# A Mamba layer between two expert layers: the convolution's input copied by ScalarE from its matmul bank to a padded SBUF buffer

## The chip, the cores and the metric

One core of a Trainium2 chip runs the whole kernel. The time is the device time of one execution, in microseconds (us). TensorE (PE) does the matmuls, VectorE (DVE) and ScalarE (ACT) the work on their results, GpSimd (POOL) some of the elementwise work, and SyncE (SP) issues most DMAs. Each engine runs its own instructions in order and waits on semaphores for the others.

## The reference, cut to what matters

Eight sequences of 256 tokens with 256 features pass through an expert layer, a Mamba layer with a small gated MLP, and the expert layer again. The part that the change touches is the depthwise causal convolution inside the Mamba layer, four taps over time for each of 512 channels:

```
zxbcdt = einsum('bld,pd->blp', h, in_proj_w)
z, x, B, C, dt = split(zxbcdt, ...)
x = repeat_kv(x)                          # 128 -> 512 channels
xc = conv(x over time, conv_w, 4 taps, 3 zeros in front) # per channel
x = silu(xc + conv_b)
# then, token by token: state = exp(dt*A)*state + dt*x*B ; y = sum(state*C)
```

## The kernel before

**Layout.** Features and channels lie on the 128 partitions, the 256 tokens of a sequence along the free dimension. The 512 channels are four groups of 128; everything before the scan is done in two halves (0 and 1) of two groups, so one instruction often covers 128x512 numbers and one tap of the convolution 128x256.

**Steps and items.** The program is unrolled into steps t = -1 to 9. A step holds, for different sequences at once, an MLP (`gum`, line 850, with `down`, line 889), the expert layer (`g` and `u`, lines 808 to 810, `down`), the scan of sequence t-1 in 32 units, and the front of the next sequence (norms, projections, convolution, softplus). In the text "the MLP stretch" is the part of a step in which `gum` items run, 35 to 52 us long, and "the expert stretch" the rest, 109 to 162 us from step 2 to step 8. The front's half 0 of the next sequence (`("x", 0, "next")`) is placed in the expert stretch, half 1 (`("x", 1, "own")`) in the following MLP stretch. There are 16 such halves; step 1 does both halves of the first sequence as well.

**The order.** `items_of(t)` makes one list of items for a step and every engine walks through this list, doing its part of each item (`late_order` holds some items back on DVE and POOL). `merge` interleaves two lists: each item gets the position (lengths of the items ahead of it) / (total length of its list), and the two lists are sorted by it. The lengths are in `SPACE` (scan units against the front) and `WEIGHT` (matmul-heavy items against all that). `near` moves an item that frees a bank ahead if too many bank uses would pass; in this list it moves only the item `om`, never a convolution item.

**Side banks.** PE writes the small products into three PSUM banks (`side`), used in turn; `last_use` makes PE wait until the third use back is over, which is what `USES` and `ENDED_BY` say. For a scan unit there are two uses: `ub` (line 983, freed by the scan, line 1352) and `unit` (line 986, freed by the multiply, line 1358). For the projection x (line 956) the use ends when all eight taps are done (semaphore `conv`).

**The convolution.** DVE does the taps straight from the bank, four in item `xc` (tap 3 without shift, line 1283, and tap 2, line 1288) and four in `xd` (taps 1 and 0, line 1288), two groups each. A late tap covers only the columns that it reaches (255, 254 or 253). Tap results accumulate in `xs`. Then ACT does the tanh of the silu (`xt`, line 1094).

**Scan units on DVE and POOL.** Item `ub` multiplies (line 1340) and `unit` scans (line 1352) and multiplies (line 1358). POOL adds each unit's result to a sum (line 1478, 128x512); behind the last unit of a group (units 7, 15, 23, 31) it makes two narrower adds more (lines 1481 and 1484, 128x256). POOL also does two multiplies for each chunk of the expert layer (`by_u`, line 1457, and `by_comb`, line 1465).

Of the kernel before, what the change touches and what calls it, by code (L numbers as in the profile page):

```python
# [33 lines left out]
P = 128  # L34
SEQ, BATCH, DM = 256, 8, 256
# [64 lines left out]
    "rt2": {"side_filled": 1, "comb_ready": 1},  # L100
    "z": {"side_filled": 1, "z_tanh": 1},
    "zm": {"z_done": 1},
    "x": {"side_filled": 1},
    "xc": {"conv": TAPS},
    "xd": {"conv": TAPS},
    "xt": {"x_tanh": 1},
# [92 lines left out]


FILLS = ("n1", "n2", "rt1", "rt2", "z", "x", "split", "dt", "ub", "unit", "outp")
ENDS = {"x": "xd", "ub": "unit", "outp": "om", "z": "zm", "split": "sr", "n1": "nc"}


def near(items):

    out, done, open_for = [], set(), {}

    def emit(it):
        if it in done:  # L210
            return
        if it[0] == "xd":
            emit(("xc",) + it[1:])
        fills = it[0] in FILLS and kind_of(it) != "n1r"
        if fills:
            for end in [e for e, n in open_for.items() if n >= SIDES - 1 and e != it]:
                emit(end)
            for end in open_for:
                open_for[end] += 1
        open_for.pop(it, None)  # L220
        done.add(it)
        out.append(it)
        if fills and it[0] in ENDS:
            open_for[(ENDS[it[0]],) + it[1:]] = 0

    for it in items:
        emit(it)
    return out
# [28 lines left out]
def items_of(t):  # L257
# [61 lines left out]
    if ln2:  # L319
# [9 lines left out]
          **{(k, w): x for w in ("lnO", "rmsO") for k, x in (("n1", 2), ("nc", 2), ("n2", 3), ("nm", 2))},  # L329
          **{(k, i, "own"): x for k, i, x in (("split", 0, 2), ("x", 0, 2), ("sr", 0, 2), ("dt", 0, 2), ("xt", 0, 2),  # L330
                                              ("split", 1, 2), ("sr", 1, 2), ("z", 0, 2), ("sp", 0, 2))}}
SPACE = {"n1": 1.4, "nc": 5, "n2": 3, "nm": 4, ("n1", "rms1"): 4, ("nm", "rms1"): 5, "rq": 0.75, "split": 1.4, "sr": 2, "sl": 2, "x": 1.4, "xc": 2, "xd": 2, "xt": 2,
         "xm": 2, "z": 1.4, "zm": 2, "dt": 2, "sp": 2, "sp_dt": 2, "sp_x": 1, "y0": 1, "ub": 2, "unit": 2, "rt1": 2,
         "yz": 0.1, "outp": 4, "om": 2, ("yz", JC - 1): 2, ("n1", "rms2"): 2}

# [91 lines left out]
def late_order(items):  # L427

    out, held, left = [], None, 0
    for it in items:  # L430
# [6 lines left out]
        else:  # L437
# [6 lines left out]
USES = {  # L444
    "side": {"n1c": [("centered", 1)], "n2": [("logged", 1)],
             "rt1": [("rt_exp", 1)], "rt2": [("comb_ready", 1)],
             "z": [("z_done", 1)], "x": [("conv", TAPS)],
             "split": [("part_rest", 1)],
             "dt": [("dt_pre", 4)], "ub": [("scanned", 1)],
             **{name: [("read_out", 1)] for name in ("unit_first", "unit", "unit_last")},  # L450
# [2 lines left out]
            "cmb": [("comb_copied", 1)]},  # L453
}

ENDED_BY = {"x": "xd", "g": "by_g", "ub": "unit", "outp": "om", "z": "zm", "split": "sr", "n1": "nc"}
BANKS = {"side": SIDES, "gub": GUBS}


# [34 lines left out]
def macaron_kernel(nc, d):  # L494
# [12 lines left out]
    with ctx:  # L507
        def sb(name, shape, dt=F32):
            return ctx.enter_context(nc.sbuf_tensor(name, shape, dt))
# [59 lines left out]
        lbuf = sb("lbuf", [P, 2, SEQ])  # L569
        tmp = sb("tmp", [P, 2, SEQ])  # L570
        dtr = sb("dtr", [P, SEQ])
        decays = sb("decays", [P, 2, 2, SEQ])
        decay = [decays[:, i, :, :] for i in range(2)]

# [99 lines left out]
        def pair(b):  # L674
            return b[:, :].rearrange("p (h s) -> p h s", h=2)
# [328 lines left out]
        def _(act):  # L1004
# [5 lines left out]
            def do(s, it):  # L1010
# [59 lines left out]
                elif kind == "y0":  # L1070
                    act.wait_ge(sem["dtx"], s.count("dtx", ("sp_x",) + it[1:], 1))
                    for j in range(2 * it[1], 2 * it[1] + 2):
                        A(y[:, j, :], xs[:, j, :], ACT.Copy, scale=vecs[:, j, 0:1]).then_inc(sem["y_init"], 1)
                elif kind == "carry":
                    act.wait_ge(sem["normed"], s.count("normed", it, 0))
                    A(hn[:], hn_next[:], ACT.Copy).then_inc(sem["carried"], 1)
                elif kind == "rt1":
                    act.wait_ge(sem["side_filled"], s.count("side_filled", it, 1))
                    A(e_sc[:], s.side_of(it)[:, 0:TT * EXPERTS].rearrange("p (a e) -> p a e", a=TT),
                      ACT.Exp, scale=-1.0).then_inc(sem["rt_exp"], 1)  # L1080
                elif kind == "z":
                    act.wait_ge(sem["side_filled"], s.count("side_filled", it, 1))
                    j = 2 * it[1]
                    if (least := s.count("y_gated", it, 0)) is not None:
                        act.wait_ge(sem["y_gated"], least)
                    A(z2[:, j:j + 2, :], pair(s.side_of(it)), ACT.Tanh,
                      scale=0.5).then_inc(sem["z_tanh"], 1)
                elif kind == "xt":
                    act.wait_ge(sem["conv"], s.count("conv", ("xd",) + it[1:], TAPS))
                    if (least := s.count("part_lo", it, 0)) is not None:  # L1090
                        act.wait_ge(sem["part_lo"], least)
                    if (least := s.count("x_done", it, 0)) is not None:
                        act.wait_ge(sem["x_done"], least)
                    A(tmp[:], xs[:, 2 * it[1]:2 * it[1] + 2, :], ACT.Tanh).then_inc(sem["x_tanh"], 1)
                elif kind == "split":
                    act.wait_ge(sem["side_filled"], s.count("side_filled", it, 1))
                    if (least := s.count("spread", it, 0)) is not None:
                        act.wait_ge(sem["spread"], least)
                    b = pair(s.side_of(it))
                    if it[1] == 0:  # L1100
                        A(dtr[:], b[:, 1, :], ACT.Copy).then_inc(sem["part_hi"], 1)
                        A(parts[:, 0, 0, :], b[:, 0, :], ACT.Copy).then_inc(sem["part_hi"], 1)
                    else:
                        for h in range(2):
                            A(parts[:, 0, h, :], b[:, h, :], ACT.Copy).then_inc(sem["part_hi"], 1)
                elif kind == "sr":
                    n = 1 if it[1] == 0 else 2
                    act.wait_ge(sem["part_rest"], s.count("part_rest", it, 1))
                    A(parts[:, 1, 0:n, :], tmp[:, 0:n, :], ACT.Copy).then_inc(sem["part_mid"], 1)
                elif kind == "dt":  # L1110
                    act.wait_ge(sem["side_filled"], s.count("side_filled", it, 1))
                    for last_read in ("dt_fix", "decay", "dtx"):
                        if (least := s.count(last_read, it, 0)) is not None:
                            act.wait_ge(sem[last_read], least)
                    b = pair(s.side_of(it))
                    for h in range(2):
                        j = 2 * it[1] + h
                        A(ubuf[:, h, :], b[:, h, :], ACT.Abs, bias=vecs[:, j, 1:2]).then_inc(sem["dt_pre"], 1)
                        A(dts[:, j, :], b[:, h, :], ACT.Relu, bias=vecs[:, j, 1:2]).then_inc(sem["dt_pre"], 1)
                    act.wait_ge(sem["dt_pre"], s.count("dt_pre", it, 4))  # L1120
                    A(ubuf[:], ubuf[:], ACT.Exp, scale=-1.0).then_inc(sem["dt_exp"], 1)
                elif kind == "sp":
                    act.wait_ge(sem["dt_exp"], s.count("dt_exp", it, 0))
                    if (least := s.count("dt_fix", it, 0)) is not None:
                        act.wait_ge(sem["dt_fix"], least)
                    A(lbuf[:], ubuf[:], ACT.Ln, bias=1.0).then_inc(sem["dt_ln"], 1)
                elif kind == "ub":
                    u = it[1]
                    j, p = u // PAIRS, u % PAIRS
                    if u % (UNITS // 2) == 0:  # L1130
                        act.wait_ge(sem["dt_fix"], s.count("dt_fix", it, 0))
                    if u == 0 and s.n == 2:
                        act.wait_ge(a_ready, 1)
                    if (least := s.count("scanned", it, 1, back=2)) is not None:
                        act.wait_ge(sem["scanned"], least)
                    for h in range(2):
                        n = 2 * p + h

                        A(decay[u % 2][:, h, 1:SEQ], dts[:, j, 1:SEQ], ACT.Exp,  # L1139
                          scale=a_neg[:, j, n:n + 1]).then_inc(sem["decay"], 1)  # L1140
# [5 lines left out]
        def _(dve):  # L1146
# [3 lines left out]
            v.memset(marks[:, :, 1:2], -2.0).then_inc(zeroed, 1)  # L1150
            for i in range(2):
                v.memset(decay[i][:, :, 0:1], 0.0).then_inc(zeroed, 1)
            dve.wait_ge(zeroed, 5)
            dve.wait_ge(a_exp, 1)
            v.tensor_scalar(a_neg[:], a_neg[:], -1.0, None, ALU.mult).then_inc(a_ready, 1)
            v.tensor_copy(sc[:, :, EXPERTS:SCW], marks[:]).then_inc(a_ready, 1)
# [4 lines left out]
            def do(s, it):  # L1161
# [104 lines left out]
                                           ALU.add, ALU.mult).then_inc(sem["z_done"], 1)  # L1266
                elif kind in ("xc", "xd"):

                    of = ("x",) + it[1:]
                    dve.wait_ge(sem["side_filled"], s.count("side_filled", of, 1))  # L1270
                    if kind == "xd":
                        dve.wait_ge(sem["conv"], s.count("conv", ("xc",) + it[1:], TAPS))
                    taps = range(TAPS - 1, TAPS // 2 - 1, -1) if kind == "xc" else range(TAPS // 2 - 1, -1, -1)
# [3 lines left out]
                    for k in taps:  # L1277
                        for h in range(2):
                            j, late = 2 * it[1] + h, TAPS - 1 - k
                            o, i = xs[:, j, late:SEQ], pair(s.side_of(of))[:, h, 0:SEQ - late]  # L1280
                            w = vecs[:, j, 3 + k:4 + k]
                            if late == 0:
                                v.tensor_scalar(o, i, w, vecs[:, j, 2:3], ALU.mult,
# [280 lines left out]
```

## Time and the profile before

| | |
|---|---|
| median of 3 runs | 1781.56 us (1778.46 to 1782.3) |
| the profiled execution | 1783.27 us, span 1781.4 us |
| PE busy | 1551.8 us, 87% of the span |
| DVE busy | 1265.5 us, 71% |
| POOL busy | 988.8 us, 56% |
| ACT busy | 843.5 us, 47% |
| granted TensorE clock, mean | 0.958 |

The span is the time from the first to the last instruction of the program. An engine's busy time is an average over stretches with different limits, so the wait views and the timelines of single stretches say more than the shares.

### The profile page before, as it was taken

To read this page: it belongs to the slowest core of one execution; us is meant where nothing else is said; L and a number is where in the kernel's file an instruction comes from. 1 tells how busy PE (TensorE), PEld (TensorE's weight loads), DVE (VectorE), ACT (ScalarE), POOL (GpSimd) and SP (SyncE) were. 2 spreads that over 40 slices of the span, in tenths; PEclk is the share of its full clock that TensorE was granted. 3 is DMA by queue.
4 is the path that set the end of the run, shared out by engine and by line. 5 is a ranking of instruction groups with operands and counts; after the bars stand their busy time and mean duration, and the time that the engine had idled before them with its cause. 6 is when DMAs were issued, how large, how long until landed. Compare 5 with 4: busy or idle time off the path is not lost. (4 is left out here: it accounts for less than half of the span.)

```text
span 1781.4 us, 22496 instructions
## 1 busy us (share of the span) xinstructions
PE 1551.8 (87%) x7088; PEld 1165.3 (65%) x7088; DVE 1265.5 (71%) x2067; ACT 843.5 (47%) x1692; POOL 988.8 (56%) x1048
## 2 busy tenths in 40 slices
PE   5998887887899889888998799879987998889979
PEld 4665554546566567666776677667765776667868
DVE  4553587876868788968797879778977787777321
ACT  4443454543555346535553466346634564444323
POOL 1663354654767457636665566447644666458525
PEclk9999999999999999999999999999998999889989
DMA  4565221123323232423232333233322333233434
GB/s 161 205 217 192 75 95 50 63 77 103 133 90 113 97 121 92 138 88 116 95 126 96 98 115 128 89 104 116 126 95 73 124 114 113 80 112 131 133 100 149
DMA packets 73430, 202.35 MB, mean 114 GB/s; under 512 B 10049, under 2 KB 22561, under 8 KB 72929
## 3 DMA queue, kind: packets, MB, share of 16 engines
q1 hardware_dynamic: 65120, 175.75, 29.6%
q0 software_dynamic: 8192, 25.17, 4.6%
q8 instruction: 57, 0.93, 0.2%
q14 instruction: 61, 0.49, 0.1%
HBM read 175.46 MB, written 25.43 MB: 113 GB/s over the span
## 5 line engine op out<-in xcount | busy, mean ns | idle before, releaser
L1478 POOL TENSOR_TENSOR ring<-ring 128x512 f32<-128x512 f32 x192 | 256.9, 1338 | 378.9 <-DVE ring L1358 378.6
L808 PE MATMUL gub<-x_hi,wr 128*128 128x384 f32 (+2 forms) x1040 | 428.9, 412 | 29.1 <-DVE hid L1175 22.4
L889 PE MATMUL acc<-hid,w_down 128*128 128x384 f32 (+2 forms) x1040 | 408.1, 516 | 15.6 <-POOL hid L1457 15.5
L1457 POOL TENSOR_TENSOR hid<-hid,u_sb 128x384 f32<-128x384 f32 (+2 forms) x260 | 292.0, 1123 | 182.2 <-ACT u_sb L1041 168.0
L810 PE MATMUL gub<-x_hi,wr 128*128 128x384 f32 (+2 forms) x1040 | 370.0, 356 | 0.0
L809 PE MATMUL gub<-x_lo,wr 128*128 128x384 f32 (+2 forms) x1040 | 369.8, 356 | 0.0
L1352 DVE TENSOR_TENSOR_SCAN ring<-decays,side 128x512 f32<-128x512 f32 x256 | 310.4, 1213 | 40.1 <-ACT decays L1139 37.3
L1051 ACT ACTIVATE hid<-gub 128x384 f32<-128x384 f32 (+2 forms) x324 | 156.6, 483 | 365.9 <-PE gub L850 189.5
L1041 ACT ACTIVATE u_sb<-gub 128x384 f32<-128x384 f32 (+2 forms) x260 | 132.2, 508 | 336.6 <-PE gub L810 336.5
L1465 POOL TENSOR_TENSOR hid<-hid,weight 128x384 f32<-128x384 f32 (+2 forms) x240 | 267.6, 1116 | 29.6 <-ACT weight L1031 15.0
L889 PEld LDWEIGHTS acc<-hid,w_down 128*128 128x128 f32 x1040 | 185.7, 192 | 110.9 <-issue 41.8
L808 PEld LDWEIGHTS gub<-x_hi,wr 128*128 128x128 f32 x1040 | 202.1, 194 | 64.5 <-issue 37.4
L1340 DVE TENSOR_TENSOR side<-dtx,side 128x512 f32<-128x512 f32 x256 | 176.7, 690 | 93.5 <-PE side L983 93.1
L1139 ACT ACTIVATE decays<-dts,a_neg 128x255 f32<-128x255 f32 x512 | 228.5, 497 | 0.1
L809 PEld LDWEIGHTS gub<-x_lo,wr 128*128 128x128 f32 x1040 | 202.7, 195 | 20.0 <-issue 6.3
L810 PEld LDWEIGHTS gub<-x_hi,wr 128*128 128x128 f32 x1040 | 201.2, 193 | 13.8
L1175 DVE SCALAR_TENSOR_TENSOR hid<-hid,gub 128x384 f32<-128x384 f32 (+2 forms) x260 | 149.1, 573 | 85.7 <-ACT hid L1051 85.6
L1358 DVE TENSOR_TENSOR ring<-ring,side 128x512 f32<-128x512 f32 x256 | 176.2, 688 | 46.1 <-PE side L986 22.6
L983 PE MATMUL side<-bst,sel_b 96*128 96x256 bf16 x512 | 100.9, 279 | 63.4 <-DVE ring L1352 46.2
L850 PE MATMUL gub<-xn_mlp,wm_gu 128*128 128x256 f32 x512 | 129.3, 402 | 4.7 <-DMA wm_gu<-in_w_mlp 3.5
L956 PE MATMUL side<-rn,w_in 128*128 128x256 f32 x448 | 118.1, 411 | 15.5 <-DVE ring L1352 13.4
L983 PEld LDWEIGHTS side<-bst,sel_b 96*128 96x128 bf16 x512 | 40.3, 99 | 133.0 <-DVE ring L1352 62.0
(117 smaller groups left out, 1856.8 us busy)
## 6 DMA issues: line engine op xcount, KB each, us to landing
wr<-w_halves SPq DMA_DIRECT2D x234, 512.0 KB, 3.3
wm_gu<-in_w_mlp POOLq DMA_DIRECT2D x64, 256.0 KB, 3.1
w_halves<-wr SPq DMA_DIRECT2D x26, 512.0 KB, 3.2
wm_down<-in_w_mlp POOLq DMA_DIRECT2D x64, 128.0 KB, 2.7
w_raw<-in_w_gu SPq DMA_DIRECT2D x26, 256.0 KB, 3.7
rows<-parts SPq DMA_DIRECT2D x16, 384.0 KB, 2.3
cst<-rows SPq DMA_DIRECT2D x48, 128.0 KB, 2.5
xin<-in_x SPq DMA_DIRECT2D x8, 256.0 KB, 3.0
```

Of the source, the lines that this page charges most:

```text
L808: mm(out, w[:, 0, half, k, :], x_hi[:, k, a:b], start=(k == 0), stop=False)
L809: mm(out, w[:, 0, half, k, :], x_lo[:, k, a:b], start=False, stop=False)
L810: last = mm(out, w[:, 1, half, k, :], x_hi[:, k, a:b], start=False, stop=(k == KC - 1))
L889: last = mm(acc[k][:, a:b], w, h[:, a:b], start=(c == 0), stop=(c == (MLP_CHUNKS if mlp else FFN_CHUNKS) - 1))
L1051: A(hid[c % HSLOTS][:, a:b], s.gub_of(it)[:, a:b], ACT.Tanh, scale=0.5).then_inc(sem["tanh_done"], 1)
L1139: A(decay[u % 2][:, h, 1:SEQ], dts[:, j, 1:SEQ], ACT.Exp, scale=a_neg[:, j, n:n + 1]).then_inc(sem["decay"], 1)
L1340: v.tensor_tensor(b, twice(dtx[:, j, :]), b, ALU.mult).then_inc(sem["driven"], 1)
L1352: v.tensor_tensor_scan(w.rearrange("p h s -> p (h s)"), decay[u % 2][:, :, :].rearrange("p h s -> p (h s)"), s.side_of(ub)[:, :], 0.0, ALU ...
L1358: v.tensor_tensor(w, w, pair(s.side_of(it)), ALU.mult).then_inc(sem["read_out"], 1)
L1457: nc.gpsimd.tensor_tensor(h, h, u_sb[c % USLOTS][:, a:b], ALU.mult).then_inc(sem["hidden"], 1)
L1465: nc.gpsimd.tensor_tensor(h, h, weight[c // 3 % CSLOTS][:, a:b], ALU.mult).then_inc(sem["weighted"], 1)
L1478: add(ysum, ysum, ring[:, ring_at(it)], ALU.add).then_inc(sem["y_sum"], 1)
```

## The change

ACT gets a new part for item `x`: it copies the bank, 128x512, to a new SBUF buffer `xpad` of 259 columns for each group, whose first three columns are set to zero once at the start. The bank's use ends with this copy (semaphore `x_padded`). DVE waits for the copy and not for the matmul, and takes all eight taps from `xpad`, each over all 256 columns with a shifted start. In the planner the length of `x` in `SPACE` goes from 1.4 to 2, and `xd` is no longer an item that `near` knows as the end of `x`.

```
-    "x": {"side_filled": 1},
+    "x": {"side_filled": 1, "x_padded": 1},
...
-ENDS = {"x": "xd", "ub": "unit", "outp": "om", "z": "zm", "split": "sr", "n1": "nc"}
+ENDS = {"ub": "unit", "outp": "om", "z": "zm", "split": "sr", "n1": "nc"}
...
-        if it[0] == "xd":
-            emit(("xc",) + it[1:])
...
-SPACE = {... "x": 1.4, ...
+SPACE = {... "x": 2, ...
...
-             "z": [("z_done", 1)], "x": [("conv", TAPS)],
+             "z": [("z_done", 1)], "x": [("x_padded", 1)],
...
-ENDED_BY = {"x": "xd", "g": "by_g", "ub": "unit", "outp": "om", "z": "zm", "split": "sr", "n1": "nc"}
+ENDED_BY = {"g": "by_g", "ub": "unit", "outp": "om", "z": "zm", "split": "sr", "n1": "nc"}
...
+        xpad = sb("xpad", [P, 2, SEQ + TAPS - 1])
...
+                elif kind == "x":
+                    act.wait_ge(sem["side_filled"], s.count("side_filled", it, 1))
+                    if (least := s.count("conv", it, 0)) is not None:
+                        act.wait_ge(sem["conv"], least)
+                    A(xpad[:, :, TAPS - 1:], pair(s.side_of(it)), ACT.Copy).then_inc(sem["x_padded"], 1)
...
-            dve.wait_ge(zeroed, 5)
+            v.memset(xpad[:, :, 0:TAPS - 1], 0.0).then_inc(zeroed, 1)
+            dve.wait_ge(zeroed, 6)
...
-                    dve.wait_ge(sem["side_filled"], s.count("side_filled", of, 1))
+                    dve.wait_ge(sem["x_padded"], s.count("x_padded", ("x",) + it[1:], 1))
...
-                            o, i = xs[:, j, late:SEQ], pair(s.side_of(of))[:, h, 0:SEQ - late]
+                            o, i = xs[:, j, :], xpad[:, h, k:k + SEQ]
```

## Rows read from the trace of the kernel before

**Rows 1.** The page: busy us of each engine, share of the span, instructions.
```profile
PE 1551.8 (87%) x7088; PEld 1165.3 (65%) x7088; DVE 1265.5 (71%) x2067; ACT 843.5 (47%) x1692; POOL 988.8 (56%) x1048
```

**Rows 2.** Windows: stretch; its length; busy PE, PEld, DVE, ACT, POOL; clock; DMA.
```profile
160.00:403.30 243.30, 193.30 (x757) 126.52 (x757) 178.72 (x272) 120.09 (x225) 118.52 (x95) 0.94 0.24 79
...
606.70:644.30 37.60, 31.17 (x139) 24.96 (x140) 29.52 (x57) 14.24 (x30) 15.75 (x30) 0.92 0.25 77
```

**Rows 3.** Waits: who <- whom: us in total, times, longest.
```profile
DVE xs L1283 <- PE side L956: 20.8, 9, 2.8
...
PE side L986 <- DVE xs L1288: 10.8, 8, 2.4
...
PE side L967 <- DVE xs L1288: 2.4, 2, 1.2
```

**Rows 4.** Instructions that touch the tile xs: the taps, ns min/median/max.
```profile
L1288 DVE SCALAR_TENSOR_TENSOR xs<-side,vecs,xs x96: 468/473/481, 189.0 to 1530.6; 128x255 f32<-128x255 f32 x32, 128x254 f32<-128x254 f32 x32, 128x253 f32<-128x253 f32 x32
L1283 DVE TENSOR_SCALAR xs<-side,vecs x32: 535/537/546, 188.1 to 1526.8; 128x256 f32<-128x256 f32 x32
```

**Rows 5.** Single lines of the kernel, ns min/median/max: kin of the changed instructions.
```profile
L1247 DVE SCALAR_TENSOR_TENSOR rn<-hn_next,lnw,rstd x16: 474/482/1510, 179.9 to 1430.6; 128x256 f32<-128x256 f32 x16
L1247 DVE SCALAR_TENSOR_TENSOR xn_mlp<-hn,lnw,rstd x16: 478/1224/1505, 396.8 to 1675.1; 128x256 f32<-128x256 f32 x16
...
L1318 DVE TENSOR_SCALAR dtx<-ubuf x16: 416/526/942, 192.9 to 1542.8; 128x512 f32<-128x512 f32 x16
...
L1086 ACT ACTIVATE z<-side x16: 597/598/601, 200.7 to 1582.3; 128x512 f32<-128x512 f32 x16
```

**Rows 6.** Timeline: taps from the bank beside POOL; start us, us, instruction.
```profile
188.20 1.28 POOL L1457 TENSOR_TENSOR hid<-hid,u_sb 128x512 f32<-128x512 f32 x1
188.97 2.62 DVE L1288 SCALAR_TENSOR_TENSOR xs<-side,vecs,xs 128x255 f32<-128x255 f32 x6
```

**Rows 7.** Timeline: two DVE instructions with two SBUF inputs beside POOL.
```profile
323.65 1.89 DVE L1247 SCALAR_TENSOR_TENSOR rn<-hn_next,lnw,rstd 128x256 f32<-128x256 f32 x2
...
323.81 1.45 POOL L1478 TENSOR_TENSOR ring<-ring 128x512 f32<-128x512 f32 x1 [2.08 <-DVE ring L1358]
325.22 1.44 POOL L1457 TENSOR_TENSOR hid<-hid,u_sb 128x512 f32<-128x512 f32 x1
```

**Rows 8.** The same two instructions apart: ns min/median/max of the pair.
```profile
L1247 DVE SCALAR_TENSOR_TENSOR rn<-hn_next,lnw,rstd x2: 479/987/1495, 323.6 to 324.0; 128x256 f32<-128x256 f32 x2
```

**Rows 9.** Timeline of the MLP stretch of step 3; in brackets the idle time before.
```profile
619.36 1.89 PE L850 MATMUL gub<-xn_mlp,wm_gu 128*128 128x256 f32 x8
...
619.96 1.26 POOL L1478 TENSOR_TENSOR ring<-ring 128x512 f32<-128x512 f32 x1 [2.57 <-DVE ring L1358]
...
624.55 0.48 PE L986 MATMUL side<-cst,sel_c 96*128 96x256 bf16 x2 [2.44 <-DVE xs L1288]
...
624.83 3.53 PE L850 MATMUL gub<-xn_mlp,wm_gu 128*128 128x256 f32 x8
...
628.81 0.42 DVE L1166 SCALAR_TENSOR_TENSOR hid<-hid,gub 128x256 f32<-128x256 f32 x1 [2.40 <-ACT hid L1051]
```

**Rows 10.** Windows around that wait; the last three columns: clock, DMA, GB/s.
```profile
619.40:621.20 1.80, 1.80 (x11) 1.59 (x10) 1.80 (x5) 0.00 (x0) 1.25 (x2) 1.00 0.00 0
624.80:628.30 3.50, 3.50 (x11) 2.64 (x10) 1.51 (x2) 0.00 (x0) 1.72 (x2) 0.52 0.01 4
```

**Rows 11.** Timeline of the expert stretch of step 4.
```profile
701.43 0.99 DVE L1283 TENSOR_SCALAR xs<-side,vecs 128x256 f32<-128x256 f32 x2 [2.28 <-PE side L956]
...
703.81 0.41 PE L808 MATMUL gub<-x_hi,wr 128*128 128x384 f32 x1 [0.98 <-DVE hid L1175]
...
705.67 1.28 POOL L1478 TENSOR_TENSOR ring<-ring 128x512 f32<-128x512 f32 x1 [3.74 <-DVE ring L1358]
...
707.02 0.73 POOL L1481 TENSOR_TENSOR ring<-ring 128x256 f32<-128x256 f32 x1
...
708.84 1.21 DVE L1352 TENSOR_TENSOR_SCAN ring<-decays,side 128x512 f32<-128x512 f32 x1
...
710.13 1.03 PE L914 MATMUL side<-sq,mean_w 128*128 128x256 f32 x4
```

More of the change, by code:

```diff
@@ L331 @@
                                               ("split", 1, 2), ("sr", 1, 2), ("z", 0, 2), ("sp", 0, 2))}}
-SPACE = {"n1": 1.4, "nc": 5, "n2": 3, "nm": 4, ("n1", "rms1"): 4, ("nm", "rms1"): 5, "rq": 0.75, "split": 1.4, "sr": 2, "sl": 2, "x": 1.4, "xc": 2, "xd": 2, "xt": 2,
+SPACE = {"n1": 1.4, "nc": 5, "n2": 3, "nm": 4, ("n1", "rms1"): 4, ("nm", "rms1"): 5, "rq": 0.75, "split": 1.4, "sr": 2, "sl": 2, "x": 2, "xc": 2, "xd": 2, "xt": 2,
          "xm": 2, "z": 1.4, "zm": 2, "dt": 2, "sp": 2, "sp_dt": 2, "sp_x": 1, "y0": 1, "ub": 2, "unit": 2, "rt1": 2,
@@ L1267, in do @@
                 elif kind in ("xc", "xd"):
-                    of = ("x",) + it[1:]
-                    dve.wait_ge(sem["side_filled"], s.count("side_filled", of, 1))
+                    dve.wait_ge(sem["x_padded"], s.count("x_padded", ("x",) + it[1:], 1))
                     if kind == "xd":
```

## The prediction

> **What bounds the kernel now.** I began with the page. PE is busy 87% of the span and DVE 71% [rows 1], so PE is the first suspect; but its work comes in order from a hand-made list, and it stands still wherever a side bank is not free. The windows by stretch show the two engines near each other in the MLP stretch: of the 37.6 us in step 3 PE is busy 31.17 and DVE 29.52 [rows 2]. So I read the view of the waits for what the convolution itself holds up. It has three entries. PE waited 10.8 and 2.4 us for the last tap before it could reuse the bank of x, together 13.2 us, 0.7% of the span; and DVE stood idle 20.8 us, in nine places, until PE had filled x [rows 3]. That is what this change can give back at first hand.
>
> The timelines show what such a place is like. In step 3 PE waits 2.44 us for the taps, then starts the next `gum` late, and DVE, which needs that product, idles 2.40 us [rows 9]. The eight matmuls of the `gum` take 3.53 us behind the wait against 1.89 before it, and the granted clock falls to 0.52 there, near the lower level (1.2 GHz), from 1.00 (2.4 GHz) [rows 9, 10]: 1.64 us more. In the expert stretch of step 4 DVE idles 2.28 us for the fill, and PE later 0.98 us for a DVE multiply that stood behind the first taps [rows 11].
>
> **The copy.** 16 copies of 128x512 from a bank, at the 0.598 us of a like ACT instruction [rows 5], are 9.6 us on an engine that is 47% busy [rows 1]. What stands behind the copy in ACT's queue reads products that PE makes after x, so it would have waited anyway. DVE starts the taps later by the copy, though, some 0.75 us with the semaphores, unless it has other work: see the order. The memset of three columns at the start and the two edits in `near` cost nothing: the memset runs before the first matmuls, and `near` never moved a convolution item.
>
> **The order.** With the length 2 every item behind x moves back. In the expert stretch of steps 2 to 6, xc goes from 36.6/78.4 = 0.467 to 37.2/79.0 = 0.471, and unit 23 stands at 30.1/64.2 = 0.469: the unit now comes between x and xc. In steps 1 and 7 the same happens with unit 24. So there the scan runs while PE fills x and ACT copies, and the copy is hidden; uncovered it would be seven times 0.75, 5.3 us. In the MLP stretch of steps 3 and 5 to 8, xd goes from 3.5/26.3 = 0.133 to 4.1/26.9 = 0.152 and passes unit 7 at 6/40.1 = 0.150. In steps 2 and 4 no unit is passed, but DVE is behind PE there anyway. Only in the first two halves of step 1 do x and xc stay neighbours: 2 x 0.75 = 1.5 us. Some later front items also move by one unit; I take nothing for them, and 5 us either way in the range.
>
> **The taps by themselves.** A tap of line 1288 takes 473 ns from the bank [rows 4]. An instruction of the same kind and width with all inputs in SBUF takes 474 to 482 undisturbed [rows 5]. 96 of them: +0.7 us. The first tap (537 ns, [rows 4]) becomes one with a single SBUF input; the nearest row is line 1318, twice as wide and 416 ns at best [rows 5]. Between 0 and 300 ns saved I take 150: 32 x 0.15 = 4.8 us, 0.3 per half.
>
> The Trainium skill ("VectorE: DVE Perf Modes", section on the TRN2 errata) gives a Vector instruction 58 cycles plus its columns from SBUF and 120 from PSUM at 0.96 GHz. By that 128 taps would save 62 cycles each, an estimated 8.3 us; the rows just named do not bear it out for the two-input form.
>
> **The taps beside POOL.** This is the term that decides. From the bank a tap reads one input in SBUF, and POOL doesn't touch it: six taps take 2.62 us while a POOL multiply runs undisturbed in 1.28 [rows 6]; the slowest of 96 took 481 ns [rows 4]. With two inputs in SBUF it is otherwise. Two instructions of line 1247, of exactly a late tap's form and back to back, took 479 and 1495 ns [rows 8]: POOL's add became ready during the first, waited for its end, and ran before the second, and the next POOL operation waited for that one [rows 7]. So each wide POOL operation that becomes ready during a run of taps costs DVE 1495 - 479 = 1.02 us and POOL some 0.2 (1.45 against 1.26 [rows 7, 9]). By width I take 0.47 for the narrow adds (0.73 of 1.28 us [rows 11], less the same 0.26 overlap) and 0.75 for expert multiplies of 384 columns.
>
> The skill ("SBUF — State Buffer", section "Who interferes with whom") says that an instruction with two SBUF inputs and a GpSimd instruction that reads SBUF exclude each other, the later one waiting in full. The trace agrees (1.02 us). At the full length of the add, 1.28, the contention below would be a quarter dearer.
>
> Now the places. (a) Expert stretch, seven halves: the taps follow directly on the last unit of a group, so POOL has three adds (two narrow) and one or two multiplies to do beside them: 0.5 (partly passed during the `by_g` multiply) + 0.47 + 0.47 + 1.05 = 2.5 us. Less 0.3 for the first taps, and less 1.1 of the 2.28 idle, which the scan fills (the rest stays, since the multiply needs PE's next product): +1.1 on DVE. What is late next is the following scan; it ended at 710.05 and PE's norm product took its bank at 710.13 [rows 11], so PE feels it. 7 x 1.1 = 7.7, less 1.0 where the 0.98 us waits fall away twice: +6.7. (b) MLP stretch of steps 3, 5 and 6: one wide add beside xc, three adds beside xd, 1.02 + 1.02 + 0.94 - 0.3 = 2.7, against the 2.40 idle that goes: +0.3 each, +0.9. In steps 7 and 8 the add beside xc is partly over: 2.2, against 0.7 of wait (what three waits of 2.44 leave of the 10.8 us for each of the other five): +3.0. (c) Steps 2 and 4: one add, 1.02 - 0.3, against a wait of 1.2 at the dt product [rows 3]: -0.5 each, -1.0. (d) The first two halves: 1.5 of copies, three multiplies and an add at 1.0, less 0.6: 4.9; PE is busy only 193 of the 243 us there [rows 2], so half, +2.5.
>
> The sum is +12.1 us if DVE's time is PE's time. DVE has 29% idle in all, so some is caught up; I take two thirds: +8. The profiled execution took 1783.27 us, 1.9 of it outside its span and 1.7 above the median of the runs; on it that is 1791, on the median of 1781.56 it is 1790.
>
> Both ends: were the taps never held up, DVE would gain 4.8 and lose 1.5, the waits of 13.2 and two clock drops of 1.64 would go: -19.8, or -13 at two thirds: 1768. Were all of the contention (17.5 + 13.3 + 2 + 4 = 37 us) on the path with nothing recovered, 1818.
>
> **The rivals.** *The stalls come back* (faster): POOL, not DVE, does the waiting, as in the many 480 ns cases of [rows 5]; x's bank is free at once, PE runs ahead through unit 7's product, and the clock drops go. It decides where fewer than about one POOL operation per run of four taps gets between. Two thirds of 13.2 + 3.3 is 11: 1771. Against it: every unit hands POOL an add right at its multiply's end [rows 9, 11], just where the taps now stand. *Nothing to see*: DVE's extra microseconds fall into its idle time and PE's waits move on to the next scan, 1781; for it speaks that PE is 87% busy [rows 1]. The copy and the early release happen in any case, so that the change does nothing is not among them. *POOL becomes late*: its operations wait for taps, some 36 times 0.2 to 0.5 us, and the expert's `down` waits for its multiplies: 15 us on top, 1805.
>
> **How the numbers follow.** What can be told from no change is about 0.2%, 3.6 us. My forecast, slower by 4 to 20 us, gets 0.48; POOL late 0.08; nothing to see 0.22; the stalls come back 0.22. So slower 0.56, same 0.22, faster 0.22. The likeliest is 1790, by itself 1785 to 1802. The range for 8 in 10 takes in no change and most of the faster case: 1772 to 1804.
>
> **What would show it.** Right: taps with medians near 480 ns but maxima above 1.4 us and a DVE busy time some 25 us up or more; no wait of PE for line 1288; the wait of 20.8 us down to a few; the copy at 0.6 us. Wrong: taps that stay under 0.5 us beside POOL, or PE's idle time down by 10 us. It would also go wrong if the moved front items shift a long wait elsewhere.

## The result and the profile after

The kernel with the change takes 1800.59 us, median of four runs (1798.52 to 1804.1), against 1780.01 (1775.76 to 1782.3) for the kernel before: ratio 1.0119, interval 1.0096 to 1.0142. It is slower by 20.6 us. The direction and the range of the prediction hold; the size is two and a half times the forecast of 8.4. The profiled execution took 1804.1 us, with a span of 1802.3, 20.9 us above that of before; its mean granted clock is 0.951 against 0.958.

The page, busy us of each engine, answers to [rows 1]:

```profile
PE 1560.0 (87%) x7088; PEld 1169.6 (65%) x7088; DVE 1296.2 (72%) x2068; ACT 855.4 (47%) x1708; POOL 993.5 (55%) x1048
```

DVE is busy 30.7 us more, ACT 11.9, POOL 4.7. PE does the same 7088 matmuls and is yet busy 8.2 us longer, at the lower mean clock: the work is the same.

The instructions that touch the taps and the copy, ns min/median/max, answer to [rows 4]:

```profile
L1292 DVE SCALAR_TENSOR_TENSOR xs<-xpad,vecs,xs x96: 471/479/1507, 190.8 to 1555.4; 128x256 f32<-128x256 f32 x96
L1287 DVE TENSOR_SCALAR xs<-xpad,vecs x32: 404/410/1442, 188.6 to 1547.6; 128x256 f32<-128x256 f32 x32
...
L1091 ACT ACTIVATE xpad<-side x16: 598/598/604, 187.9 to 1544.1; 128x512 f32<-128x512 f32 x16
```

The medians hardly moved, but the slowest late tap went from 481 to 1507 ns. The same groups by line, with their busy us and mean ns in front of the last bar and the idle time before them behind it:

```profile
L1292 DVE SCALAR_TENSOR_TENSOR xs<-xpad,vecs,xs 128x256 f32<-128x256 f32 x96 | 65.1, 730 | 0.6
...
L1287 DVE TENSOR_SCALAR xs<-xpad,vecs 128x256 f32<-128x256 f32 x32 | 22.5, 745 | 6.0 <-ACT xpad L1091 6.0
```

And the same lines of the kernel before:

```profile
L1288 DVE SCALAR_TENSOR_TENSOR xs<-side,vecs,xs 128x255 f32<-128x255 f32 (+2 forms) x96 | 40.1, 473 | 0.1
...
L1283 DVE TENSOR_SCALAR xs<-side,vecs 128x256 f32<-128x256 f32 x32 | 15.9, 539 | 20.8 <-PE side L956 20.8
```

Together 87.6 us busy, where the lines of the kernel before have 56.0: 31.6 more. By their mean durations the taps are 96 x 0.730 + 32 x 0.745 = 93.9 us, by the medians above 96 x 0.479 + 32 x 0.410 = 59.1: 34.8 us of the durations are waiting, inside the taps. Not all of it is in taps with two SBUF inputs: the 32 first taps, which have one tensor in SBUF and two scalars for each partition, have 32 x (0.745 - 0.410) = 10.7 us of it. From the bank, with the same scalars, the slowest of them took 546 ns [rows 4], and here 1442.

The waits answer to [rows 3]; the first two lines are the kernel before, the others the kernel after:

```profile
PE side L983 <- DVE ring L1352: 46.2, 32, 4.4
DVE ring L1358 <- PE side L986: 22.6, 31, 1.9
...
PE side L982 <- DVE ring L1356: 64.2, 38, 3.9
DVE ring L1362 <- PE side L985: 35.1, 38, 2.6
...
DVE xs L1287 <- ACT xpad L1091: 6.0, 2, 3.1
```

PE's 13.2 us for the taps are gone and DVE's 20.8 us for the fill are down to 6.0 us for the copy. But PE now waits 64.2 us for the scans, 46.2 before, and DVE's multiplies behind the scans wait 35.1 us for PE, 22.6 before. The wait has moved one bank on.

**One place of it.** The timeline of the MLP stretch of step 5, which shows the most of it:

```profile
994.62 1.22 DVE L1356 TENSOR_TENSOR_SCAN ring<-decays,side 128x512 f32<-128x512 f32 x1
...
1000.32 1.21 DVE L1356 TENSOR_TENSOR_SCAN ring<-decays,side 128x512 f32<-128x512 f32 x1
...
1000.88 1.03 PE L888 MATMUL acc<-hid,wm_down 128*128 128x256 f32 x4
...
1001.63 0.69 DVE L1362 TENSOR_TENSOR ring<-ring,side 128x512 f32<-128x512 f32 x1
...
1002.24 3.62 DVE L1292 SCALAR_TENSOR_TENSOR xs<-xpad,vecs,xs 128x256 f32<-128x256 f32 x4
1002.41 1.43 POOL L1482 TENSOR_TENSOR ring<-ring 128x512 f32<-128x512 f32 x1 [2.85 <-DVE ring L1362]
1002.62 0.38 PE L985 MATMUL side<-cst,sel_c 96*128 96x256 bf16 x2
1002.84 1.89 PE L849 MATMUL gub<-xn_mlp,wm_gu 128*128 128x256 f32 x8
1003.92 0.79 POOL L1485 TENSOR_TENSOR ring<-ring 128x256 f32<-128x256 f32 x1
1004.85 0.72 POOL L1488 TENSOR_TENSOR xs<-xs,ring 128x256 f32<-128x256 f32 x1
...
1005.78 0.41 DVE L1171 SCALAR_TENSOR_TENSOR hid<-hid,gub 128x256 f32<-128x256 f32 x1
...
1007.34 1.22 DVE L1356 TENSOR_TENSOR_SCAN ring<-decays,side 128x512 f32<-128x512 f32 x1
1008.62 0.60 PE L982 MATMUL side<-bst,sel_b 96*128 96x256 bf16 x2 [3.89 <-DVE ring L1356]
...
1009.02 1.91 PE L888 MATMUL acc<-hid,wm_down 128*128 128x256 f32 x4
```

Unit 7's multiply (1001.63) makes POOL's three adds ready at the moment when DVE starts the four taps of `xd`. They run by turns, tap, add, tap, add, tap, add, tap, and the four taps take 3.62 us (1.67 where no add is ready, as an experiment shows below). PE has its bank early and does the next `gum` at once (1002.84), but the multiply that consumes it (line 1171) stands behind the taps, and scan 8 behind that. PE is done at 1004.73 and waits 3.89 us for that scan, where the kernel before waited 2.44 for the taps, in step 5 as in step 3. Scan 6 starts at 994.62 here and scan 7 at 1000.32. Windows of this stretch (all of it, the `gum`, and the 3 us behind the wait; the clock is the third number from the end):

```profile
983.40:1023.50 40.10, 32.14 (x141) 25.61 (x140) 31.47 (x54) 14.86 (x31) 16.61 (x29) 0.88 0.23 72
1002.20:1004.70 2.50, 2.50 (x13) 1.81 (x11) 2.50 (x4) 1.85 (x5) 2.21 (x2) 1.00 0.00 0
1008.60:1011.60 3.00, 2.98 (x10) 2.20 (x11) 2.81 (x5) 0.00 (x0) 0.57 (x2) 0.50 0.00 1
```

And the same stretch before, with PE's wait for the taps and the `gum` behind it:

```profile
972.90:1008.10 35.20, 28.77 (x139) 23.37 (x139) 28.87 (x55) 14.25 (x30) 14.98 (x29) 0.98 0.26 82
...
990.78 0.39 PE L986 MATMUL side<-cst,sel_c 96*128 96x256 bf16 x2 [2.44 <-DVE xs L1288]
991.01 1.89 PE L850 MATMUL gub<-xn_mlp,wm_gu 128*128 128x256 f32 x8
```

The stretch is 4.9 us longer, and 3.4 of them are PE's matmuls themselves: behind the idle 3.89 us the clock is granted at 0.50, the lower level of 1.2 GHz, and four matmuls that take 1.03 us at 1000.88 take 1.91 at 1009.02. Behind the shorter wait of this stretch in the kernel before the clock had not fallen: the `gum` at 991.01 takes 1.89 us.

**The expert stretch of step 4**, answering to [rows 11]:

```profile
708.16 1.70 DVE L1287 TENSOR_SCALAR xs<-xpad,vecs 128x256 f32<-128x256 f32 x2
...
708.33 1.39 POOL L1482 TENSOR_TENSOR ring<-ring 128x512 f32<-128x512 f32 x1 [0.46 <-DVE ring L1362]
...
709.79 4.99 DVE L1292 SCALAR_TENSOR_TENSOR xs<-xpad,vecs,xs 128x256 f32<-128x256 f32 x6
...
717.37 0.39 PE L982 MATMUL side<-bst,sel_b 96*128 96x256 bf16 x2 [1.49 <-DVE ring L1356]
```

Eight taps take 6.7 us, where a half took 56.0 / 16 = 3.5 before, and PE again waits for the scan behind them.

**Where the 20.9 us lie.** Stretches from the first `gum` matmul of a step to its first other matmul into a `gub` bank (the expert layer's, line 861 or 807 after), and from there to the next `gum`, in the two profiled executions. PE's matmuls are the borders, so a few us can pass from one row to its neighbour. By these borders the MLP stretch of step 6 is 32.6 us long before, shorter than the 35 given ahead. Of the seven halves of (a) the first, in step 1, lies in the first row.

| stretch | predicted, before the discount | measured |
|---|---|---|
| up to step 2, first two halves, (d) | +2.5 | -1.9 |
| MLP of steps 2 and 4, (c) | -1.0 | -1.1 |
| MLP of steps 3, 5 and 6, (b) | +0.9 | +7.3 |
| MLP of steps 7 and 8, (b) | +3.0 | +1.5 |
| seven expert stretches, (a) | +6.7 | +15.3 |
| the rest | 0 | -0.2 |
| sum | +12.1 | +20.9 |

### The profile page after: what moved, and what is told of

It is laid out like the page before. It is cut to its first block and busy times, and to the rows that moved or that the text cites. A ratio compares the mean times of both kernels' runs of the same rounds, so it can differ in the third digit from the quotient of the medians.

```text
span 1802.3 us, 22528 instructions
## 1 busy us (share of the span) xinstructions
PE 1560.0 (87%) x7088; PEld 1169.6 (65%) x7088; DVE 1296.2 (72%) x2068; ACT 855.4 (47%) x1708; POOL 993.5 (55%) x1048
## 5 line engine op out<-in xcount | busy, mean ns | idle before, releaser
L888 PE MATMUL acc<-hid,w_down 128*128 128x384 f32 (+2 forms) x1040 | 413.0, 521 | 15.6 <-POOL hid L1461 15.5
L1362 DVE TENSOR_TENSOR ring<-ring,side 128x512 f32<-128x512 f32 x256 | 176.1, 688 | 58.2 <-PE side L985 35.1
L982 PE MATMUL side<-bst,sel_b 96*128 96x256 bf16 x512 | 102.2, 282 | 86.7 <-DVE ring L1356 64.2
```

Source lines behind the costliest of these rows:

```text
L888: last = mm(acc[k][:, a:b], w, h[:, a:b], start=(c == 0), stop=(c == (MLP_CHUNKS if mlp else FFN_CHUNKS) - 1))
L1362: v.tensor_tensor(w, w, pair(s.side_of(it)), ALU.mult).then_inc(sem["read_out"], 1)
```

## The experiments

The change has four separable parts: the copy and early release, the taps from SBUF, the order given by the length 2, and what the order does to `xd` in particular. All runs below were timed in rounds beside the kernel before; ratios are to it. My theory at the outset was that the taps' meeting with POOL costs the time, whatever the order; the rival, that the moved items do.

**The old length.** The change with the planner's length as before.

```
-SPACE = {... "x": 2, ...
+SPACE = {... "x": 1.4, ...
```

> The changed kernel with the length of x back at 1.4, so that every item keeps its place from before; copy, early release and taps from SBUF stay. If the taps' meeting with GpSimd is what costs (theory), little changes: 1793 to 1803 us, the taps still some 85 us busy. If the moved items cost (rival order), most of the 20 us goes: 1780 to 1787. If the copy's delay costs (rival copy), it gets worse than 1800, since the copy stands uncovered in front of the taps, with about 0.75 us more idle in each of some nine places: 1805 or more.

1786.33 us, ratio 1.0017 (0.9999 to 1.0036): nearly all of the loss is gone with one number of the planner. My theory fell here. Its rows show that the taps still meet POOL (53.3 + 18.3 = 71.6 us busy, 56.0 from the bank) and that the copy is now uncovered:

```profile
L1292 DVE SCALAR_TENSOR_TENSOR xs<-xpad,vecs,xs 128x256 f32<-128x256 f32 x96 | 53.3, 609 | 0.1
...
L1287 DVE TENSOR_SCALAR xs<-xpad,vecs 128x256 f32<-128x256 f32 x32 | 18.3, 612 | 26.6 <-ACT xpad L1091 26.6
```

DVE stands 26.6 us before the first taps, more than the 20.8 of the kernel before, and still the time is that of before.

**Taps that cannot meet POOL.** In the kernel after and in the kernel before, each tap becomes a memset of 300 columns into a scratch tile, so the convolution is left out; the waits, the copy and the order stay.

```
-v.scalar_tensor_tensor(o, i, w, o, ALU.mult, ALU.add).then_inc(sem["conv"], 1)
+v.memset(junk[:, h, :], 0.1).then_inc(sem["conv"], 1)
```

> The changed kernel with each tap replaced by a memset of 300 columns into a scratch tensor (the convolution is left out), about 0.37 us each and with no input in SBUF; copy, early release, order and waits stay. Read it against e5_before_memsets. Theory (contention): without the meeting the change costs nothing and the early release shows, so e3 is 0 to 12 us below e5. Rivals order and copy: e3 stays 12 us or more above e5.

> The kernel before with the same memsets in the place of its taps (the convolution is left out), waits and order as before: the control for e3_memsets. All theories: vector work is some 18 us less, so 1766 to 1778 us.

```profile
L1290 DVE MEMSET junk<- x128: 308/308/308, 186.1 to 1519.1; 128x300 f32 x128
```

1765.58 us (0.9904, 0.9875 to 0.9933) with the change and 1769.48 (0.993, 0.9905 to 0.9955) without it. With taps that take 308 ns whatever POOL does, the change is worth 3.9 us by the medians or nothing (the intervals overlap), and no loss. So without the meeting there is no loss from order and copy, in a kernel whose DVE also has shorter taps and so more room; a later run keeps the taps at their length. By stretches of the two profiled executions the change still moves time here: the expert stretches of steps 2 to 8 are 8.7 us longer with it and the MLP stretches 7.5 shorter.

**The same memsets with the old length.**

```
-SPACE = {... "x": 2, ...     # in the memset kernel with the change
+SPACE = {... "x": 1.4, ...
```

> As e3_memsets (the convolution is left out, memsets in the place of the taps), but with the length 1.4. Theory (the moved order costs because it brings the taps to GpSimd's adds): without the meeting the two orders are alike, 1761 to 1770, within 5 us of e3. Rival (the moved order costs by itself, since the scan's items come later for it): 1745 to 1757, lower than e3 by about what the length cost with taps.

1763.68 us, 0.9887 (0.985 to 0.9925), 0.17% or 3 us below the run with length 2 by the ratios, which their intervals don't tell apart. The moved order is harmless without the contention and dear with it: the loss is a product of the two.

**The early release undone.** Old length, taps from the copy, but the bank is held until the last tap.

```
-"x": [("x_padded", 1)],
+"x": [("conv", TAPS)],       # and ENDED_BY with "x": "xd" again
```

> The changed kernel with the length 1.4 and the bank of x held until the last tap, as before: only the copy and the taps from SBUF are left of the change. Read it against e2_old_length, which differs in the release alone. Theory: the early release is worth something by itself, 5 to 13 us, so 1800 to 1812 here. Rival (the release is worthless, because tensor engine's wait only moves to the next scan): within 3 us of e2.

1806.8 us, 1.0131 (1.0103 to 1.0159). Against the old-length run with the release that is 20 us, more than I expected. PE's waits for the taps are back, larger than the 13.2 of before, since the taps are longer:

```profile
PE side L985 <- DVE xs L1292: 21.9, 12, 3.2
PE side L966 <- DVE xs L1292: 5.1, 3, 2.2
```

So in the old order the release gains what the slower taps cost, and the two cancel.

**The new order in one kind of stretch only.**

```
+("x", 0, "next"): 1.4,      # first run: length 2 only in the MLP stretch
+("x", 1, "own"): 1.4,       # second run: length 2 only in the expert stretch
```

> The changed kernel with the length 1.4 for the half that stands in the expert stretch and 2 for the one in the MLP stretch: only the MLP order has moved. By stretches, the run with the old length is some 23 us shorter than the changed kernel in the MLP stretches and 4 us longer in the expert ones. Theory (the cost is the last taps being moved behind unit 7, in the MLP stretch): 1797 to 1806. Rival (the taps behind units 23 and 24 in the expert stretch cost it): 1780 to 1788.

> The other half of it: length 2 in the expert stretch, 1.4 in the MLP stretch. Theory: 1777 to 1787, about the run with the old length. Rival: 1796 to 1806.

1809.15 us, 1.0154 (1.0104 to 1.0204), with the new order in the MLP stretch; 1784.89, 1.0019 (0.9995 to 1.0044), with it in the expert stretch. The first is above the 1806 that the theory allowed and no lower than the whole change; the second is in the theory's range. The loss belongs to the MLP stretch's order. Step 5 of the second run, where `xd` stands ahead of unit 7 again:

```profile
984.72 1.21 DVE L1356 TENSOR_TENSOR_SCAN ring<-decays,side 128x512 f32<-128x512 f32 x1
...
990.42 1.67 DVE L1292 SCALAR_TENSOR_TENSOR xs<-xpad,vecs,xs 128x256 f32<-128x256 f32 x4
...
992.00 1.21 DVE L1356 TENSOR_TENSOR_SCAN ring<-decays,side 128x512 f32<-128x512 f32 x1
...
993.36 1.10 PE L966 MATMUL side<-dtr,w_dt 128*128 128x256 f32 x4 [1.35 <-DVE ring L1356]
...
994.10 1.27 POOL L1482 TENSOR_TENSOR ring<-ring 128x512 f32<-128x512 f32 x1 [3.72 <-DVE ring L1362]
...
995.49 1.22 DVE L1356 TENSOR_TENSOR_SCAN ring<-decays,side 128x512 f32<-128x512 f32 x1
...
996.76 0.39 PE L982 MATMUL side<-bst,sel_b 96*128 96x256 bf16 x2 [0.35 <-DVE ring L1356]
```

The taps run while POOL has nothing to do (1.67 us), POOL's adds run beside products and scans, scan 8 starts 3.49 us behind scan 7 instead of 7.02, and PE waits 1.35 us for scan 7 and 0.35 for scan 8, instead of nothing and 3.89. The window of the stretch:

```profile
973.50:1008.40 34.90, 29.14 (x141) 23.44 (x140) 29.63 (x56) 14.86 (x31) 15.42 (x29) 0.98 0.27 83
```

**Which of the moved items.** The length 2 moves `xd` and everything behind it. One run puts `xd` back ahead of unit 7 and leaves the later items late; the other moves `xd` alone.

```
+("x", 1, "own"): 1.4, ("xd", 1, "own"): 2.6,   # later items late, xd as before
+("xd", 1, "own"): 1.4,                         # xd late, later items as before
```

> The changed kernel with the last two taps of the MLP stretch back ahead of unit 7, while the softplus and silu items behind them stay as late as the change put them. Theory (the taps beside unit 7's three adds cost): 1780 to 1789. Rival (the later softplus and silu items cost, for they too have two inputs in SBUF or sit before the scan's products): 1796 to 1806.

> The opposite: of the items of the MLP stretch only the last two taps stay behind unit 7, the later items go back. Theory: 1794 to 1804. Rival: 1780 to 1789. If both runs lie between, the two share it.

1790.94 us, 1.0056 (1.004 to 1.0072), 2 us above the theory's range and 5 below the rival's, and 1802.31, 1.0111 (1.0081 to 1.014), as the theory had it. `xd` alone behind unit 7 gives the whole loss. Against the expert-order run, in which nothing of the MLP stretch is moved, it costs 0.92%, 16 us; the later items alone cost 0.37%, 7 us. With both moved the ratio is 1.0119, so the two don't add up; why was not followed. In the three MLP stretches of steps 3, 5 and 6, moving `xd` alone costs 14.4 us between the two profiled executions (40.0, 40.1 and 33.7 us against 34.9, 34.9 and 29.6).

**The adds taken away from those taps.** The changed kernel, with POOL's three adds behind unit 7 made one column wide, so that most of that group's sum is left out.

```
+few = 1 if u == PAIRS - 1 else SEQ
-add(ysum, ysum, ring[:, ring_at(it)], ALU.add)
+add(ysum[:, :, 0:few], ysum[:, :, 0:few], ring[:, ring_at(it), :, 0:few], ALU.add)
...
```

> The changed kernel, but GpSimd makes the three adds of unit 7 on one column in the place of 256 (the sum of that group is left out, so the output is wrong); order, waits and all else stay. Theory (these three adds between the taps cost): taps xd of the MLP stretch take about 1.9 us in the place of 3 to 3.9, and the time falls by 8 us or more, to 1785 to 1793. Rival (place in the order, not the meeting): 1797 to 1803.

1788.21 us, 1.0037 (1.0022 to 1.0052): 0.8% better than the change, with the order untouched. The same place in step 5:

```profile
984.57 1.21 DVE L1356 TENSOR_TENSOR_SCAN ring<-decays,side 128x512 f32<-128x512 f32 x1
...
992.18 1.67 DVE L1292 SCALAR_TENSOR_TENSOR xs<-xpad,vecs,xs 128x256 f32<-128x256 f32 x4
992.36 0.36 POOL L1483 TENSOR_TENSOR ring<-ring 128x2 f32<-128x2 f32 x1 [2.85 <-DVE ring L1362]
...
995.33 1.22 DVE L1356 TENSOR_TENSOR_SCAN ring<-decays,side 128x512 f32<-128x512 f32 x1
...
996.61 0.39 PE L982 MATMUL side<-bst,sel_b 96*128 96x256 bf16 x2 [1.93 <-DVE ring L1356]
```

From the start of scan 6 to that of scan 8 this kernel needs 10.76 us (984.57 to 995.33), the expert-order run 10.77 (984.72 to 995.49), the change 12.72 (994.62 to 1007.34). The difference, 1.96 us, is what the three adds cost the four taps (3.62 - 1.67 = 1.95). That joins the two experiments: `xd` behind unit 7 is bad mainly because three adds are ready there. The adds are not all of it. PE still waits 1.93 us for scan 8, and in steps 3 and 6 the stretches are 36.9 and 31.3 us, 2.0 and 1.7 longer than in the expert-order run; in step 3 the clock falls there too (a `gum` of 3.54 us). Against the kernel before, the three stretches of steps 3, 5 and 6 are together 7.3 us longer with the change, 2.4 shorter with the narrow adds and 6.1 shorter in the expert-order run: 9.7 us go with the adds, and 3.7 stay with the later place. The narrow adds also take some 1.8 us of work from POOL in each step, which this run does not separate; PE's wait for POOL's `hid` multiply is 15.5 us with them as without.

**Half of the change.** The copy for half 1 alone (MLP stretch), old length; half 0, which lies in the expert stretch, takes its taps from the bank as before.

```
-"x": [("x_padded", 1)],
+"x": [("conv", TAPS)], "x1": [("x_padded", 1)],   # x1: half 1
...
+if not it[1]:
+    o, i = xs[:, j, late:SEQ], pair(s.side_of(of))[:, h, 0:SEQ - late]
```

> The change for the half in the MLP stretch alone (copy, early release, taps from SBUF), with the length 1.4; the other half's taps read the bank as before. By the stretches of the run with the old length, MLP stretches gained some 16 us and expert stretches lost 19. Theory (the release pays where the scan bounds and the meeting with GpSimd costs where its queue is full): 1764 to 1776, faster than both kernels. Rival (the loss in the expert stretch is only what the MLP stretch pushed ahead of it): 1778 to 1788.

1779.23 us, 0.9973 (0.9954 to 0.9993): the time lies in the rival's range and not in the 1764 to 1776 of the theory. It is a gain, small and only just told from no change, and of the versions that leave no work out the only one faster than both kernels. Its profiled execution is on the low side of its ten runs (1773.68); in it the MLP stretches of steps 2 to 8 are 11 us shorter than before and the expert stretches 1 us longer. Against the run with the old length, from which it differs in half 0 alone, it is 0.44% or 8 us faster, and against the expert-order run, which also has half 0's items moved, 0.46%: that is what half 0's copy and contended taps cost beyond what their early release gives.

**ScalarE does a tap instead of a copy.** The kernel before, with the first tap made by ACT from the bank into `xs`; DVE does the other three from the bank, so no tap reads two SBUF inputs.

```
+elif kind == "xc":
+    A(xs[:, j, :], pair(s.side_of(of))[:, h, :], ACT.Identity,
+      bias=vecs[:, j, 2:3], scale=vecs[:, j, 2 + TAPS:3 + TAPS])
...
-taps = range(TAPS - 1, TAPS // 2 - 1, -1)
+taps = range(TAPS - 2, TAPS // 2 - 1, -1)
```

> A try at something better, from the kernel before: ScalarE makes the first tap with the bias from the bank into xs, two instructions of some 0.47 us in the place of the copy, and DVE the other three from the bank, which stays held till the end. No tap has two inputs in SBUF; DVE loses 32 x 0.537 = 17 us. Theory: no meeting with GpSimd, shorter hold of the bank: 1765 to 1777. Rival (the chain matmul, ScalarE, VectorE is longer in front of the taps and the bank is held as long as before): 1778 to 1788.

1779.17 us, ratio 1.0 (0.9985 to 1.0015): nothing gained, as the rival had it, where the theory forecast at least 1777. It takes 32 first taps from DVE, 15.9 us of busy time, and DVE waits 10 us more than the 20.8 of [rows 3], now for ACT's tap:

```profile
DVE xs L1298 <- ACT xs L1096: 30.8, 9, 3.9
```

## Why the prediction was right and wrong

**Right: the contention and its price.** Taps from SBUF take turns with POOL. The four taps of `xd` lost 3.62 - 1.67 = 1.95 us to the three adds; the prediction's 1.02 + 0.94 is 1.96. By the mean durations of each stretch, less the medians above, the taps lost 2.9 us a half in steps 3, 5 and 6 (2.98 forecast), 1.0 in steps 2 and 4 (1.02), 1.3 in steps 7 and 8 (2.2), 3.3 to 3.8 in five expert halves, 0.9 in a sixth and 1.4 in the seventh, in step 1 (2.5 forecast for each). With the 2.3 of the first two halves (4 forecast) that is 34.8 us, against 37. What the prediction had too narrow is the condition, two inputs in SBUF: 10.7 of the 34.8 us are in the first taps, which have one. The sum did not feel it, since it counts POOL operations by place. The rule of the Trainium skill ("SBUF — State Buffer", section "Who interferes with whom") that DVE and GpSimd lock each other out of a shared pair of ports is borne out by the turns; a wait in full is not, since three adds of 1.27 + 0.73 + 0.72 us (their times in the expert-order run) cost 1.95 and not 2.72. The copy (598 ns), the late taps (479 ns) and the end of both waits came as forecast, and DVE's busy time is up 30.7 us, where "some 25 us up or more" was named as the sign.

**Near, in part by luck.** Steps 2 and 4 (-1.1 against -1.0, but as +0.3 and -1.5 and not as -0.5 each) and, within the borders' accuracy, steps 7 and 8 (+1.5 against +3.0).

**Wrong: step (b), `xd` behind unit 7.** "2.7, against the 2.40 idle that goes: +0.3 each" books the direct cost rightly and a credit that the same move takes away. The bank's release does give about 2 us a half in steps 3, 5 and 6: with `xd` ahead of unit 7 these three stretches are 6.1 us shorter than before in the expert-order run. With `xd` behind it PE is handed its bank, runs through the `gum`, and then stands 3.89 us at the next bank, whose scan is queued behind the contended taps; and the clock falls behind that wait, in step 3, where it did behind the old wait too, and in step 5, where it did not. PE waits 3.9 us for scan 8 in all three steps. The result was +7.3 instead of +0.9 (-0.1, +4.8 and +2.6), and the order's own price in these three halves 13 to 14 us, of which the narrow adds give back 9.7. The prediction asked what is late next for the expert stretch and not here.

**Wrong: two thirds.** "DVE has 29% idle in all, so some is caught up" took 4 us off. The share is an average; where the taps stand, DVE is busy 31.47 of 40.10 us, and PE waits for scans in 38 places, 64.2 us. DVE's idle time fell by only 9.8 us (1781.4 - 1265.5 to 1802.3 - 1296.2) while its busy time rose by 30.7.

**Wrong in size: the expert stretch, (a).** +15.3 in the profiles against +6.7. The expert-order run has +11.0 there and half of the change +1.0, so 10 us go with half 0's part in the profiles, 8 by the times, near the 6.7. But the run with the old length has +19.2 there, with 4 us less in the MLP stretches, for the same 8 us by the times, and the memset kernels have +8.7 without any contention. So these stretches also take what the MLP stretches gain, and not all of the 15.3 is the taps'. The term's own sum takes 1.0 off for two waits of 0.98 us; twice that is 2.0. The rest came with the moved items of the MLP stretch (with `xd` alone moved, the expert stretches are +16.4) and with the later front items: "I take nothing for them, and 5 us either way", where they cost 7 us alone. How much each has of the 15.3 stays open.

**Wrong without effect: the copy's cover.** Uncovered, the copy was to cost 5.3 us. The old length uncovers it (26.6 us of waits) and the time is the same as with it covered (1.0017 and 1.0019). And (d) was +2.5 against -1.9.

**The rivals.** *The stalls come back* needed few POOL operations beside the taps; that is what the order of before gives in the MLP stretch, and half of the change has a part of that gain, 0.27%. *Nothing to see*, with the waits moving to the next scan, describes the old length, 1.0017. *POOL becomes late* was not seen: POOL gained 4.7 us of busy time, and PE's wait for its `hid` multiply is 15.5 us before and after.

## What to carry to other kernels

Moving an operand from PSUM to SBUF to free a bank changes what an instruction meets: from the bank no tap here waited for GpSimd, from SBUF the taps lost 34.8 us to it. So look in the timeline at what GpSimd has ready at that very place, and price each operation there before you count the freed bank as a gain. A bank that is freed early pays only if the next wait of the same engine is not for something queued behind the instructions that became slower, so follow the queue to the next bank and not only to the next engine. And when a change brings a planner constant along with a mechanism, time each alone: here one constant was worth 1%, and half of the mechanism at the old constant was the only version that gained with no work left out.

## What the runs showed of the hardware

A waiting POOL operation gets in between each two DVE instructions that use two SBUF inputs, even when these are queued back to back: three adds met by four taps, one between each two (3.62 us against 1.67). A `tensor_scalar` with one tensor in SBUF waits as well: beside POOL's 128x512 add two first taps take 1.70 us, and the slowest of 32 took 1442 ns where the median is 410 and none from the bank took over 546.

The one-input tap is 127 ns cheaper from SBUF than from the bank (410 against 537 ns), the two-input tap is not cheaper at all (479 against 473 for one to three columns fewer). The estimate from the Trainium skill's figure ("VectorE: DVE Perf Modes", section on the TRN2 errata) is 65 ns for each, which neither form shows; it leaves out that the page divides the columns by a multiplier of the mode.

The early release of a bank was worth less than the waits named for it: it gained 20 us where PE had waited 27.0 for the taps. With memsets of 308 ns in the place of the taps PE had waited 8.1 us for them, and the whole change gained no more than 4 us.
